# The last two combination chunks moved later, the last one written out by a plain store

## The reference

```python
xn = layernorm(x)
s = attention(xn)   # 32 heads of 8, window of 16 keys, each score times its mask weight, softmax, projection + bias
g = silu(moe(xn))   # each token to the best of 8 experts, plus a shared gated feed-forward network
x = x + s * g
```

## Time and profile before

| | |
|---|---|
| median of 3 runs | 599.69 us (599.25 to 600.19) |
| the profiled execution's own time | 600.95 us |
| its span, first to last instruction | 599.1 us |
| PE busy | 546.0 us (91%) |
| DVE busy | 439.2 us (73%) |
| POOL busy | 255.5 us (43%) |
| ACT busy | 240.3 us (40%) |
| mean granted TensorE clock | 0.976 |

### The profile page before, as it was taken

How to read it: one execution, slowest core, us unless ns; L and a number is a source line. 1 busy time by engine, 2 the same in 40 slices (tenths; PEclk the granted TensorE clock), 3 DMA queues, 4 the chain that set the end, 5 groups by cost and what they waited for, 6 DMA issues and landing times.

```text
span 599.1 us, 10330 instructions
## 1 busy us (share of the span) xinstructions
PE 546.0 (91%) x3302; PEld 474.1 (79%) x3302; DVE 439.2 (73%) x1029; ACT 240.3 (40%) x506; POOL 255.5 (43%) x188
## 2 busy tenths in 40 slices
PE   1989999979988999999999999999999999898952
PEld 1757789858867899989899988899879788786941
DVE  6777858898768557566566466646899999999862
ACT  1464454536652443442433433342535434352210
POOL 7133324038885223223323322320476795974630
PEclk9989999989998999999999999999999999999977
DMA  9624534235625666766566756563235664754421
GB/s 302 208 80 156 187 106 124 88 96 176 186 95 166 202 188 200 217 189 197 174 189 199 219 175 204 156 171 102 44 63 74 92 89 60 104 76 64 70 44 19
DMA packets 106345, 83.17 MB, mean 139 GB/s; under 512 B 42164, under 2 KB 104500, under 8 KB 106164
## 3 DMA queue, kind: packets, MB, share of 16 engines
q1 hardware_dynamic: 90180, 64.81, 36.9%
q0 software_dynamic: 10496, 12.59, 12.7%
q10 hardware_dynamic: 5616, 5.11, 2.5%
HBM read 59.41 MB, written 27.26 MB: 145 GB/s over the span
## 4 chain that ended last, share of the span: by engine, by line
PE 60%; DVE 13%; POOL 8%; issue 6%; DMA 5%; ACT 4%; SPq 1%; ACTq 0%; POOLq 0%; DVEq 0%
PE psV L939 11%; PE psM L989 11%; PE psS L914 8%; PE psM L998 5%; PE psM L966 5%; PE psM L925 4%; PE psM L961 4%; PE psM L889 4%; DMA xnT<-ys_dram,slot 4%; PE psM L894 3%; POOL xnT L442 3%; POOL Sx L432 3%; PE psM L947 2%; DVE O L760 2%; DVE Sx L708 2%
## 5 line engine op out<-in xcount | busy, mean ns | idle before, releaser
L432 POOL TENSOR_TENSOR Sx<-Sx,mx 128x752 f32<-128x752 f32 x64 | 100.6, 1571 | 122.5 <-DVE mx L718 122.1
L939 PE MATMUL psV<-VB,PTs 128*128 128x132 f32 x1024 | 134.8, 285 | 17.8 <-DVE O L760 17.6
L939 PEld LDWEIGHTS psV<-VB,PTs 128*128 128x128 f32 x1024 | 129.2, 195 | 22.4 <-issue 21.0
L426 POOL TENSOR_TENSOR Sx<-Sx,cst 128x752 f32<-128x752 f32 x28 | 47.0, 1677 | 183.4 <-DVE Sx L708 183.4
L914 PE MATMUL psS<-kBD,qBD 128*128 128x188 f32 x512 | 97.8, 323 | 0.2 <-DVE Sx L708 0.2
L914 PEld LDWEIGHTS psS<-kBD,qBD 128*128 128x128 f32 x512 | 84.7, 190 | 9.6 <-issue 2.5
L740 DVE STREAM_TRANSPOSE PTs<-Sx 128x512 f32<-128x512 f32 x128 | 82.8, 685 | 4.2 <-ACT Sx L497 4.2
L708 DVE TENSOR_TENSOR Sx<-psS,cst 128x752 f32<-128x752 f32 x64 | 60.0, 938 | 30.6 <-PE psS L914 30.2
L989 PE MATMUL psM<-xT,EB 128*128 128x128 f32 x624 | 76.5, 276 | 0.6 <-DMA EB<-in_L_ffn_up_w 0.6
L760 DVE TENSOR_TENSOR O<-psV,rs 32x128 f32<-32x128 f32 x256 | 73.5, 287 | 4.8
L989 PEld LDWEIGHTS psM<-xT,EB 128*128 128x128 f32 x624 | 73.8, 192 | 3.0 <-ACT qBD L486 1.3
(11 more groups left out here) (106 smaller groups left out, 688.6 us busy)
## 6 DMA issues: line engine op xcount, KB each, us to landing
EB<-in_L_ffn_gate_w SPq DMA_DIRECT2D x39, 256.0 KB, 3.1
EB<-in_L_ffn_up_w SPq DMA_DIRECT2D x39, 256.0 KB, 3.6
EB<-in_L_ffn_down_w SPq DMA_DIRECT2D x39, 256.0 KB, 3.0
VB<-v_dram SPq DMA_DIRECT2D x256, 32.0 KB
stage<-xs_dram SPq DMA_DIRECT2D x39, 128.0 KB, 2.2
ys_dram<-yb ACTq DMA_DIRECT2D x39, 128.0 KB, 3.1
xs_dram<-blank SPq DMA_DIRECT2D x9, 512.0 KB, 3.2
v_dram<-vS SPq DMA_DIRECT2D x8, 512.0 KB, 3.0
```

The lines of the kernel that those rows point to most:

```text
L432: nc.gpsimd.tensor_tensor(s, s, mx[n % 3][:, :].unsqueeze(2).broadcast_to([P, 2 * G, KW]), ALU.subtract).then_inc(a_sub, 1)
L939: last = mm(psV[:, j, at:at + HS * VW], PTs[n % 2][:, k, j, i, :], VB[n % 2][:, i, k, :, VW * j:VW * j + VW], start=k == 0, stop=k == 1)
```

## The change

What it does:

- silu of chunk 14 goes from step 61 to 63, its result from 62 to 65. Its gather goes from step 60 to 62 and its accumulating store from 63 to 66.
- silu of chunk 15 goes from step 62 to 66 (ahead of attention of tile 31 in that step); its gather goes from step 61 to 65.
- the shared product of tiles 30 and 31 (`sd` 61) goes from step 61 to step 64, behind `weighted` of unit 62 and ahead of `output` of tile 30. ScalarE's copy of it moves to step 64, behind exps of 63.
- chunk 15 is not added onto `out` in DRAM. In step 40 SyncE loads its 256 rows of `x` into `XR`, a part of `EB` where the experts' weights lay; after result of chunk 15 VectorE adds it to `XR` (128x512), and SyncE writes `XR` to `out` by a plain DMA. The last preset leaves those rows out.

```diff
@@ -133,8 +133,10 @@
     found += [("xc", i) for i in pair_at(n, 2)]
     found += [("xb", i) for i in pair_at(n, 1)]
     found += [("xa", i) for i in pair_at(n, 0)[:1]]
-    if n < U and n % UB < 6:
+    if n < U and n % UB < 6 and n != U - 3:
         found.append((("sg", "su", "sg", "su", "sd", "sd")[n % UB], n))
+    if n == U:
+        found.append(("sd", U - 3))
     found += [("xa", i) for i in pair_at(n, 0)[1:]]
     if 1 <= n < BATCH:
         found += [("v", t) for t in range(n * BT, n * BT + BT)]
@@ -144,11 +146,13 @@
 
 
 def silu_at(n):
-    return [c for c in range(NC) if max(C_STEP + 1 + c * 4 // 3, 2 * BT * (c // 2) + 5 + c % 2) == n]
+    last = {NC - 2: U - 1, NC - 1: LAST}
+    return [c for c in range(NC) if last.get(c, max(C_STEP + 1 + c * 4 // 3, 2 * BT * (c // 2) + 5 + c % 2)) == n]
 
 
 def result_at(n):
-    return [c for c in range(NC) if max(C_STEP + 2 + c * 4 // 3, 4 * c + 6) == n]
+    last = {NC - 2: U + 1, NC - 1: LAST}
+    return [c for c in range(NC) if last.get(c, max(C_STEP + 2 + c * 4 // 3, 4 * c + 6)) == n]
 
 
 ORDER = [job for n in range(-1, LAST + 1) for job in jobs_of(n)]
@@ -215,6 +219,7 @@
         etab = EB[:, at:at + NT * E].rearrange("p (t e) -> p t e", e=E)
         at += NT * E
         rcst = EB[:, at:at + C_END - C_STAY]
+        XR = EB[:, 3 * CT * C:4 * CT * C]
         Y = [EB[:, i * CT * C:(i + 1) * CT * C] for i in range(3)]
 
         ident = cst[:, C_ID:C_ID + P]
@@ -251,7 +256,7 @@
         b_wg = [sem(f"b_wg{i}") for i in range(2)]
         b_xT, b_et, b_ea, b_hT, b_y = (sem("b_" + n) for n in ("xT", "et", "ea", "hT", "y"))
         d_y, d_st = ([sem(f"d_{n}{i}") for i in range(3)] for n in ("y", "st"))
-        d_t, d_w, d_g, d_pre = (sem("d_" + n) for n in ("t", "w", "g", "pre"))
+        d_t, d_w, d_g, d_o, d_x, d_pre, d_end = (sem("d_" + n) for n in ("t", "w", "g", "o", "x", "pre", "end"))
 
         x_tiles = x.rearrange("(t p) c -> p t c", p=P)
         out_v = out.rearrange("(t p) c -> p t c", p=P)
@@ -356,7 +361,7 @@
                 sp.dma_start(stage[:, i % 4, :], xs_dram[i * P:(i + 1) * P, :]).then_inc(b_in[i % 4], 16)
 
             def preset(k):
-                rows = slice(k * NTOK // 8, (k + 1) * NTOK // 8)
+                rows = slice(k * NTOK // 8, min((k + 1) * NTOK // 8, NTOK - CT * P))
                 sp.dma_start(out[rows, :], x[rows, :]).then_inc(d_pre, 16)
 
             for n in range(LAST + 1):
@@ -364,6 +369,9 @@
                     spread_v(n - 1)
                 if ROUTE <= n < ROUTE + 8:
                     preset(n - ROUTE)
+                if n == C_STEP:
+                    full(sp, ("xc", NX - 1))
+                    sp.dma_start(XR.rearrange("p (t c) -> p t c", t=CT), x_tiles[:, T - CT:T, :]).then_inc(d_x, 16)
                 for i in range(2 * n - 4, 2 * n - 2):
                     if 0 <= i < 10:
                         fill(i)
@@ -386,8 +394,11 @@
                 if 0 <= n - 1 <= BATCH:
                     spread_v(n - 1)
             sp.wait_ge(d_pre, 16 * 8)
+            sp.wait_ge(d_o, 1)
+            sp.dma_start(out_v[:, T - CT:T, :], XR.rearrange("p (t c) -> p t c", t=CT)).then_inc(d_end, 16)
+            sp.wait_ge(d_end, 16)
             for b in range(3):
-                sp.wait_ge(d_st[b], 16 * len(range(b, NC, 3)))
+                sp.wait_ge(d_st[b], 16 * len(range(b, NC - 1, 3)))
 
         @block.gpsimd
         def _(pool):
@@ -458,8 +469,6 @@
                     gather(c)
                 for c in result_at(n - 1):
                     add_out(c)
-            for c in result_at(LAST):
-                add_out(c)
 
         @block.scalar
         def _(act):
@@ -798,6 +807,10 @@
                 dve.wait_ge(a_s, CT * c + CT)
                 dve.wait_ge(d_w, c + 1)
                 stt(s, shared_rows(t).rearrange("p t c -> p (t c)"), 0.5, s, ALU.mult, ALU.mult).then_inc(d_g, 1)
+                if c == NC - 1:
+                    dve.wait_ge(d_x, 16)
+                    dve.wait_ge(d_g, c + 1)
+                    tt(XR, s, XR, ALU.add).then_inc(d_o, 1)
 
             moments(0)
             variance(0)
```

## The result

The change made the kernel faster by more than twice what was forecast: 594.44 us (median of 7 executions, 592.45 to 597.03) against 599.57 (7 executions of the kernel before), a ratio of 0.9918 (0.989 to 0.9947). The forecast was 597.4, with a range of 595.4 to 599.6. In two later sets of executions, on two chips, the same kernel gave 0.9913 (0.9893 to 0.9933) and 0.9925 (0.9902 to 0.9948). A ratio is that of the means, with its 95% interval, so it isn't quite the quotient of the medians.

The account below looks back on a forecast made before the run. VectorE's progress through units 62 and 63, the stretch from weighted of 62 to the last result, and the last store set the end. Product's end 580.55 plus 16.3 us gave span 596.85, 2.25 less, so 597.4 us (595.4 to 599.6).

Parts of the forecast that it names:

- those 3.5 us: Program's end: time from the last store's landing at 595.6 to the span's end at 599.1, taken as fixed.
- What bounds the kernel: Steps 60 to 66: VectorE's progress through units 62 and 63, the stretch to the last result, and the last store.
- Part 1, VectorE's order: Steps 60 to 63: weigh of 63 starts at 570.6 instead of 574.38, weighted of 62 at 575.25, 3.8 us earlier.
- The slacks: ScalarE's exps of 61 and 62 are ready 1.5 us or more before flipped needs them.
- Part 2, chunk 14 in its new place (nothing): Chunk 14's later gather, silu and store cost nothing; its store, issued near 585, lands before the plain store.
- Part 3, the product: The product behind weighted of 62 is a cost; the gather path follows it, 1.2 us beyond that through weighted of 63.
- te: End of the product behind weighted of 62: 579.15 at full clock, 580.55 with one low stretch.
- the path through the gather: From the product's end through copy, chunk 15's gather, tanh, silu and attention to the last result: 9.3 us.
- Part 4, the store: Chunk 15: accumulating DMA (4.3 us) and 0.3 removed; add 0.69 + 0.03, issue 0.2, plain store 2.6 (2.2 to 3.9) added.
- Part 5, the clock: TensorE idles 3.3 us before weighted of 62; a low clock stretch then costs 1.4 us on weighted and product.
- The gather path isn't the last: Rival, 0.04: chunk 14's accumulating store ends it, landing by 591.5; 1 us less gained from the plain store, 598.
- The clock's two rivals: Clock doesn't fall in the gap: 596.0 us (0.20); clock low through all of weighted and product: 599.5 us (0.15).

Follow-up runs that it names:

- two plain stores: The changed kernel with chunk 14 too added on VectorE and stored by SyncE's plain DMA: 592.99 us, ratio 0.9902 to the kernel before.
- the tiny DMA: The changed kernel plus a GpSimd DMA of 1 KB of zeros to an unused DRAM row, SyncE waiting for it too: 595.44 us, ratio 0.9934.

## Why the prediction was wrong

The direction and the chain were right, the size was not, and one step failed: "I take those 3.5 us as fixed." They don't belong to the last landing, whoever's DMA it is; they are the rest of GpSimd's DRAIN behind the landing of GpSimd's own last DMA. Behind SyncE's last landing it was 2.0 us in the changed kernel, because chunk 14's DRAIN still ran, and 0.3 where that too was early.

*What bounds the kernel.* Right up to the store. The chain of waits of the kernel before ends in a piece of POOLq at L162 (1.24 us from 591.25), and SyncE's waits from 590 on are two, the last landing and then 3.3 us at the program's end:

```profile
SPq L390 <- DMA out<-X: 21.0, 1, 21.0
SPq L162 <- PEq L162: 3.3, 1, 3.3
```

Both pointed to the program's end; the prediction doesn't use them.

*Part 1, VectorE's order.* Right, to within 0.4 us: weigh of 62 and 63 at 565.54 and 570.84, weighted of 62 at 575.49 after 3.21 us of idle time. The slacks held. But it is worth little here. The store alone gives 0.9921 and the whole change 0.9913 to 0.9925: with a plain store for chunk 15 alone, the new order adds nothing that can be measured. One reason is where chunk 14's store went. In the old order GpSimd's last store starts 14 us before the plain one; in the new one 4 us before it (586.92 against 590.88), and its DRAIN then ends the kernel 1.8 us behind SyncE. What VectorE's order wins is given back at the end of the chain, part by the product and part by the DRAIN. With both out of the way (two plain stores, the product in step 61) the same order of the chunks comes to 0.986 and 0.9842, clear of the 0.9921 of the store alone.

*Part 2, chunk 14 in its new place (nothing).* Half right: the gather and the silu cost nothing, the store does. The prediction has that it "lands before the plain store", which it did (591.4 against 593.0), and took that for the end of its cost. It also has it issued near 585; it was issued at 586.92, and by its DRAIN the 1.9 us counted: from 585 the DRAIN would have been over with SyncE's wait.

*Part 3, the product.* te was 580.95 against 580.55, and the path through the gather 9.1 us against 9.3 (from 580.95 to the end of result at 590.01). Its distance to the path through weighted of 63 was 2.0 us (output of 31 over at 586.82, attention at 588.86); the prediction's own terms give 1.8 (579.15 + 8.1 against 585.5), not the 1.2 that stands there. In the kernel before, the gathers of chunk 15 had landed at 571.9, 19 us ahead of the last store, not 17. That the product and then the gathers have no cover is right; removing it from there shows in the times only once the DRAIN is out of the way: nothing clear with one plain store (0.991), and 0.986 and 0.9842 against 0.9902 with two.

*Part 4, the store.* 2.1 us to landing where I took 2.6, just under my lower bound of 2.2. The prediction dwelt on the 4.3 us of the accumulating DMA against the 2.6 estimated from the Trainium skill's page DMA: Bandwidth & Descriptors, section Anatomy of one DMA, for a DMA of GpSimd; the accumulating one cost 4.5 in the profile after. That section of the Trainium skill has a fixed part of about 2.0 us, and GpSimd's plain 1 KB, which took 2.1 here, agrees with it. Missing from that comparison was the larger difference: 3.3 us of DRAIN behind either.

*Part 5, the clock.* The low stretch was there, 0.97 us longer for weighted and 0.72 for the product than at full clock, 1.7 together against the 1.4 taken. In the windows of the changed kernel (us, busy by engine, granted clock, DMA) the clock is a mixture of its two levels, 1.2 and 2.4 GHz, for weighted and for the product:

```profile
575.40:578.60 3.20, 3.11 (x17) 3.14 (x18) 2.31 (x5) 1.08 (x2) 0.00 (x0) 0.65 0.00 1
578.50:580.95 2.45, 2.45 (x10) 2.06 (x9) 1.74 (x7) 0.00 (x0) 0.00 (x0) 0.74 0.00 0
```

Between 576.5 and 578.5 alone it is 0.50. It isn't in every execution: the full clock, to which the prediction gave 0.20, came in four of the nine traces with this gap.

*The sum.* Counted from weigh of 61, to leave out what scatters ahead of the changed steps, the span was to shrink from 599.1 - 560.3 = 38.8 by 2.25; it shrank to 595.0 - 560.67 = 34.3, by 4.5. Of the 2.2 us more, 1.5 are the end behind the landing (2.0 instead of 3.5), 0.5 the landing (2.1 instead of 2.6), 0.2 the chain. With 4.5 us off, the forecast would have been 595.2, beside the measured 594.44; what is left lies within the scatter.

*The rivals.* "The gather path isn't the last" came nearest and was dismissed with 0.04: chunk 14's accumulating store did end the kernel, but through its DRAIN and with a gain greater than forecast. The clock's two rivals were about how long weighted and product take, and the miss lay elsewhere.

*Shown and not shown.* That the end is GpSimd's DRAIN is shown: by the store alone, by the two plain stores, by the tiny DMA, which but for SyncE's wait for it changes nothing else, and by the order of events in all fourteen traces: in each the span ends within 0.5 us of the later of the two, the DRAIN's end or SyncE's last wait. What the DRAIN waits for in its 3.3 us past the landing isn't known. What the clock's low stretch costs in the median isn't settled; between traces of the changed kernel, from weigh of 60 to the end, it is 39.6 and 39.2 us with it and 37.8 without.

## What to carry to other kernels

Ask what each engine still does at the program's end. Here a kernel isn't over when its last result has landed if GpSimd's last DMA landed less than 3.3 us earlier: let SyncE make the last stores, and let GpSimd's last DMA land at least that long before theirs. And undo each part of a change alone before its worth is told: here the order alone brought 2.2 us and the store alone 5.2, and both together 4.7 to 5.5, because they shorten the same end.

## What the runs showed of the hardware that was not expected

GpSimd's DRAIN at the end ran until 3.2 to 3.4 us behind the landing of its last DMA, for an accumulating store of 256 KB (4.2 to 4.5 us to landing, DRAIN 7.5 to 7.8 from its start) as for a plain one of 1 KB (2.1 and 5.4) and for a gather (3.2, in the four versions with two plain stores). A plain store of 256 KB by SyncE landed in 2.1 us where GpSimd's store was over or nearly so; it took 3.0 in the one trace with one plain store and the product in step 61, where chunk 14's store was under way for most of it. That the one slowed the other is likely, and not tested:

```profile
out<-X POOLq DMA_DIRECT2D x1, 256.0 KB, 4.3
out<-EB SPq DMA_DIRECT2D x1, 256.0 KB, 3.0
```

The executions of one kernel differ by some 3 us well ahead of the changed steps: weigh of 60 started between 552.47 and 555.37 in two traces of the changed kernel. In 599 us a gain of 1 us is better read from the trace, counted from a point behind that scatter, than from medians.
